# Gate and up products in float32r with second weights fetched per tile, in an attention plus mixture-of-experts kernel

## The reference

```python
x = x + layernorm(attention(layernorm(x)))      # 16 heads of 16, rope on q and k, softmax, Wo
x = x + layernorm(moe(layernorm(x)))
# moe: 8 experts, 2 per token, the two with the LARGEST distance to their centroid
d2 = |xs|^2 + |centroid|^2 - 2 xs @ centroid.T ; dist = sqrt(max(d2, 1e-12))
w, sel = top_k(dist, 2); w = softmax(w)
out += we[:, e] * ((silu(xs @ Wg[e] + bg[e]) * (xs @ W1[e] + b1[e])) @ W2[e] + b2[e])
```

## Time and profile before

| what | value |
|---|---|
| median of the three timed runs | 1595.93 us (1580.72 to 1603.84) |
| the profiled execution | 1573.55 us |
| its span, first to last instruction | 1571.8 us |
| mean granted TensorE clock | 0.96 |
| PE busy | 1435.0 us (91%) |
| DVE busy | 1110.0 us (71%) |
| ACT busy | 846.7 us (54%) |
| POOL busy | 431.5 us (27%) |
| DMA | 141.80 MB, mean 90 GB/s |
| attention groups | about 110 to 791 us of the span |
| output projection | about 794 to 876 us |
| routing | about 876 to 930 us |
| expert tiles | about 930 to 1515 us |
| end | about 1515 to 1572 us |

### The profile page before, as it was taken

The page is one execution under the profiler, slowest core; times in us unless marked ns, Lnnn a source line. Parts: engine busy times, 40 slices in busy tenths (PEclk is TensorE's granted clock), DMA queues, the critical chain, the costliest instruction groups (busy, mean ns, idle before and its releaser), DMA issues.

```text
span 1571.8 us, 29999 instructions
## 1 busy us (share of the span) xinstructions
PE 1435.0 (91%) x9435; PEld 792.5 (50%) x9436; DVE 1110.0 (71%) x1983; ACT 846.7 (54%) x1613; POOL 431.5 (27%) x417
## 2 busy tenths in 40 slices
PE   7899999999999999999999259999999999999950
PEld 5454333333333333333355136777777777777740
DVE  6989999999999999997037764555545555555425
ACT  4523888888888888887856322222222222222215
POOL 5750000000000010001024143444444444444425
PEclk9999999999999999999999659999999999999985
DMA  6986364334636454640458804222221222222236
GB/s 205 263 222 116 77 170 97 60 73 75 100 57 123 65 90 65 102 70 26 148 90 205 281 25 96 33 30 33 33 33 31 33 33 31 33 33 33 32 88 197
DMA packets 125116, 141.80 MB, mean 90 GB/s; under 512 B 55131, under 2 KB 98949, under 8 KB 125030
## 3 DMA queue, kind: packets, MB, share of 16 engines
q1 hardware_dynamic: 109126, 121.98, 33.7%
q0 software_dynamic: 15904, 18.66, 7.5%
HBM read 86.30 MB, written 54.30 MB: 89 GB/s over the span
## 4 chain that ended last, share of the span: by engine, by line
PE 79%; DVE 7%; issue 5%; ACT 4%; POOL 2%; DMA 1%; SPq 1%; DVEq 0%; POOLq 0%; ACTq 0%
PE psum L1687 21%; PE psum L1525 17%; PE psum L1551 16%; PE psum L1706 12%; PE psum L1697 3%; PE psum L1618 2%; DVE mx L955 2%; PE psum L1537 2%; ACT work L1344 1%; PE psum L1616 1%; PE psum L1499 1%; ACT weights L1354 1%; PE psum L1485 1%; PE psum L1673 1%; PE psum L1637 1%
## 5 line engine op out<-in xcount | busy, mean ns | idle before, releaser
L955 DVE TENSOR_REDUCE mx<-psum 128x1 f32<-128x1024 f32 x512 | 621.8, 1222 | 19.1 <-PE psum L1525 16.7
L1344 ACT ACTIVATE work<-psum 128x512 f32<-128x512 f32 x1024 | 556.4, 597 | 80.6 <-PE psum L1537 18.1
L1525 PE MATMUL psum<-stack 48*128 48x512 f32 x1024 | 372.9, 445 | 6.6 <-DVE mx L955 6.1
L1537 PE MATMUL psum<-stack 50*128 50x512 f32 x1024 | 375.4, 446 | 0.0
L1687 PE MATMUL psum<-weights,values 128*128 x1136 | 341.1, 453 | 0.6 <-DVE values L1174 0.6
L1551 PE MATMUL psum<-work,values 128*32 128x256 f32 x4096 | 328.6, 393 | 9.2 <-ACT weights L1354 9.2
L1687 PEld LDWEIGHTS psum<-weights,values 128*128 128x128 f32 x1136 | 211.3, 191 | 99.6 <-issue 3.1
L1525 PEld LDWEIGHTS psum<-stack 48*128 48x128 f32 x1024 | 151.3, 185 | 217.1 <-DVE mx L955 183.6
L1421 ACT ACTIVATE values<-values 128x342 f32<-128x342 f32 x142 | 69.3, 488 | 250.5 <-DVE values L1186 250.5
L1706 PE MATMUL psum<-weights,work 114*128 (+1 forms) x852 | 198.6, 383 | 1.2 <-ACT work L1432 0.8
L1551 PEld LDWEIGHTS psum<-work,values 128*32 128x32 f32 x4096 | 82.2, 108 | 197.2 <-ACT work L1344 101.2
(11 more groups left out here) (184 smaller groups left out, 1185.4 us busy)
## 6 DMA issues: line engine op xcount, KB each, us to landing
stack<-qk_scr SPq DMA_DIRECT2D x192, 128.0 KB, 6.2
qk_scr<-weights SPq DMA_DIRECT2D x16, 1024.0 KB, 4.8
weights<-in_w SPq DMA_DIRECT2D x8, 1368.0 KB, 6.6
ot_scr<-weights SPq DMA_DIRECT2D x16, 512.0 KB, 3.2
weights<-in_w SPq DMA_DIRECT2D x8, 684.0 KB
work<-in_b SPq DMA_DIRECT2D x8, 684.0 KB, 8.8
y_d<-zeros SPq DMA_DIRECT2D x1, 4224.0 KB, 14.0
v_scr<-weights SPq DMA_DIRECT2D x32, 128.0 KB, 2.4
```

What stands on the lines that cost most here:

```text
L955: dve.tensor_reduce(mx[:, r, a, t:t + 1], bank(4 + 2 * a, 2), AX, ALU.max, negate=True).then_inc(s_max, 1)
L1344: act.activation(pt[u % 4][:, j, :], bank((c + HG * u + n) % 3), ACT.Exp, scale=SC).then_inc(s_exp, 1)
L1525: ins = pe.matmul(bank(4 + 2 * a + half), qs[t3][at:at + QROWS, r, P * t:P * (t + 1)], ks[t3][at:at + QROWS, r, 512 * half:512 * (half + 1 ...
L1537: pe.matmul(bank((t3 + HG * u + n) % 3), ks[t3][at:at + MROWS, r, P * st:P * (st + 1)], qs[t3][at:at + MROWS, r, 512 * half:512 * (half + ...
```

## The change

1. **Gate and up in float32r.** x and the weights are each split into a high float32r part and a low remainder; a product is the sum of three: high x high, high x low, low x high. A tile has 3 chunks of 456 columns x 2 k blocks x 3 products: 18 float32r instructions. The bias is folded in: the last row of the weights is subtracted from all others, and since the 256 entries of x add up to zero its place is free for the bias; POOL sets the last column of `xn2` to 1 (`set_ones`). DVE's bias operations go away.
2. **Splitting the weights.** In the attention groups SP loads one expert's raw weights every second group (`load_raw`), POOL splits them (`split_weights`, after every odd group's `copy_values`), and SP stores the first six experts' parts to DRAM (`park`), from where they are loaded again during output projection, routing and the first tiles (`load_w1`, now 2.8 MB each).
3. **Second weights per tile.** They are packed into `w2_d` in DRAM and one expert's 768 KB block is fetched for each tile into one of two buffers (`stream_w2`).
4. **Transfers** of row counts that are not multiples of 16 are split into a multiple of 16 and a rest.
5. **Tile loops** of DVE, ACT and POOL are written out; the indirect DMAs read their index columns in place; there are two `x_row` and two `y_row` buffers; all of x2 comes back during the tiles.

```diff
+CG = 2 * HID // 3
+TAIL = HID - CG
+WSIZE = 2 * KC * 2 * HID
+JOBS = (3, 4, 5, 6, 7, 2, 0, 1)
+PARKED = 6
...
+        def load_raw(sp, n):
+            e = JOBS[n]
+            after(sp, s_wl, KC * n)
+            sp.dma_start(raw[:, 0, :], w1[e, 0:P, :]).then_inc(s_raw, 16)
+            for lo, hi in ((0, P - 16), (P - 16, P - 1)):
+                sp.dma_start(raw[lo:hi, 1, :], w1[e, P + lo:P + hi, :]).then_inc(s_raw, 16)
+            sp.dma_start(raw[P - 1:P, 1, :], b1[e].rearrange("(a n) -> a n", a=1)).then_inc(s_raw, 16)
+            sp.dma_start(raw[:, 2, :], w1[e, C - 1, :].partition_broadcast(P)).then_inc(s_raw, 16)
+        def park(sp, n):
+            sp.wait_ge(s_wh, KC * (n + 1))
+            sp.wait_ge(s_wl, KC * (n + 1))
+            after(sp, s_park, 16 * n)
+            sp.dma_start(w1_d[n], w1_sb[:, n % 2]...).then_inc(s_park, 16)
+        def stream_w2(sp, t, q):
+            e = sp.value_load(tile_e[0:1, bass.ds(t, 1)], min_val=0, max_val=E - 1)
+            if not isinstance(t, int) or t > 1:
+                sp.wait_ge(s_yp, t - 1)
+            sp.dma_start(w2_sb[q]..., w2_d[bass.ds(e, 1), :, :]...).then_inc(s_w2[q], 16)
...
             # SP, attention group g
                 if more:
                     load_max_rows(sp, i, c + 1, 0)
+                if g > 1 and g % 2 == 0 and g // 2 - 1 < PARKED:
+                    park(sp, g // 2 - 1)
...
                 if more:
                     load_max_rows(sp, i, c + 1, 1)
+                if g % 2 == 0:
+                    load_raw(sp, g // 2)
+                else:
+                    pack_w2(sp, g // 2)
...
             for u in range(NT // 2):
-                keep(u)
...
+                keep(u)                  # now waits for set_ones(u)
+                if u == 8:
+                    sp.wait_ge(s_vg, NG)
+                    load_w1(sp, 2)
             sp.wait_ge(s_x2, NT // 2)
-            sp.dma_start(x2_d...[:, kept:, :], x2[:, kept:, :]).then_inc(s_x2s, 16)
+            sp.dma_start(x2_d..., x2).then_inc(s_x2s, 16)
             sp.wait_ge(s_op, NT // 2)
-            for e in range(E - 3, E - 1):
-                load_w1(sp, e)
+            for n in range(2):
+                load_w1(sp, n)
             sp.wait_ge(s_x2s, 16)
-            for e in range(early):
-                load_b1(sp, e)
+            sp.wait_ge(s_dd, 1)
+            load_w1(sp, 3)
             sp.wait_ge(s_wc, 1)
             sp.dma_start(w_d[0:2 * NTOK, :]..., w_turned).then_inc(s_wd, 16)
...
+            def split_weights(n):                               # POOL
+                high, low = w1_sb[:, n % 2, 1], w1_sb[:, n % 2, 0]
+                pool.wait_ge(s_raw, 80 * (n + 1))
+                after(pool, s_park, 16 * (n - 1))
+                pool.tensor_tensor(raw[:, 0, :], raw[:, 0, :], raw[:, 2, :], ALU.subtract).then_inc(s_sub, 1)
+                pool.tensor_tensor(raw[0:P - 1, 1, :], raw[0:P - 1, 1, :], raw[0:P - 1, 2, :], ALU.subtract).then_inc(s_sub, 1)
+                for k in range(KC):
+                    pool.wait_ge(s_sub, KC * n + k + 1)
+                    pool.tensor_copy(high[:, k, :], raw[:, k, :]).then_inc(s_wh, 1)
+                for k in range(KC):
+                    pool.wait_ge(s_wh, KC * n + k + 1)
+                    pool.tensor_tensor(low[:, k, :], raw[:, k, :], high[:, k, :].bitcast(F32), ALU.subtract).then_inc(s_wl, 1)
...
                 if not (isinstance(g, int) and g + 2 >= NG):
                     copy_values(i, c + 2)
+                if g % 2 == 1:
+                    split_weights(g // 2)
                 if g in (9, 13):
                     norm_o((g - 9) // 4)
...
+            for t in range(NS):                                 # POOL, tiles
+                if t + 2 < NS:
+                    gather(t + 2)        # rows, then weights
+                if t > 0:
+                    scatter(t - 1)
...
+            def hidden(t):                                      # DVE
+                dve.wait_ge(s_si, 2 * t + 2)
+                after(dve, s_ht, t)
+                dve.tensor_tensor(hid[:, 0:TAIL], bank(1)[:, TAIL:CG], gates[:, 0:TAIL], ALU.mult).then_inc(s_hid, 1)
+                dve.wait_ge(s_gu, 3 * t + 3)
+                dve.tensor_tensor(hid[:, TAIL:HID], bank(2)[:, 0:CG], gates[:, TAIL:HID], ALU.mult).then_inc(s_hid, 1)
...
             def gate_up(t, e):                                  # PE
                 pe.wait_ge(s_mx, t + 1)
+                for c in range(3):
+                    ...
+                    dst = bank(c)[:, 0:CG]
+                    at = CG * c
                     for k in range(KC):
+                        for n, (x_part, w_part) in enumerate(((x_high, 1), (x_high, 0), (x_low, 1))):
+                            last = pe.matmul(dst, x_part[:, k, :],
+                                             w1_sb[:, bass.ds(e, 1), w_part, k, at:at + CG]...,
+                                             start=k + n == 0, stop=k + n == KC + 1)
                     last.then_inc(s_gu, 1)
```

More of the change, by code:

```diff
@@ L305, in build @@
         c = Carve(weights)
+        x2_back = c.take([NT, C])
+        c.at = 2 * WSIZE
         y_all = c.take([NT, C])
+        w1_d = nc.dram_tensor("w1_d", (PARKED, P, WSIZE), F32, kind="Internal").ap()
+        w2_d = nc.dram_tensor("w2_d", (E, P, KH * C), F32, kind="Internal").ap()
         x2_d = nc.dram_tensor("x2_d", (NTOK, C), F32, kind="Internal").ap()
@@ L864, in _ @@
             pool.wait_ge(s_wd, 32)
[L865 removed]
+            for t in range(2):
                 gather(t)
[L867 to L873 removed]
+            for t in range(NS):
[3 more added lines that the diff above has]
+                    scatter(t - 1)
+            scatter(NS - 1)
             def finish(u, p):
                 pool.wait_ge(s_fn, 2 * u + 2)
[L877 removed]
+                both = [v[:, bass.ds(2 * u, 2), :] for v in (y_all, x2_back)]
                 pool.tensor_tensor(both[0], both[0], both[1], ALU.add).then_inc(s_fo, 1)
@@ L1431, in save_ht @@
                 after(act, s_yp, t)
-                act.activation(h_t.rearrange("p k t -> p (k t)")[0:KP, 0:4 * P], bank(4)[0:KP, :], ACT.Copy).then_inc(s_hta, 1)
-            gate(0)
-            save_ht(0)
-            gate(1)
-            save_y(0)
-            save_ht(1)
-            with act.Fori(2, NS) as t:
+                act.activation(h_t.rearrange("p k t -> p (k t)")[0:KP, 0:4 * P], bank(4)[0:KP, :], ACT.Copy).then_inc(s_hts, 1)
+            for t in range(NS):
                 gate(t)
-                save_y(t - 1)
+                if t > 0:
+                    save_y(t - 1)
                 save_ht(t)
@@ L1698, in turn_hidden, with down @@
                 last.then_inc(s_ht, 1)
-            def down(t, e):
-                pe.wait_ge(s_hta, t + 1)
-                pe.wait_ge(s_htd, t + 1)
+            def down(t, q, loads):
+                pe.wait_ge(s_hts, 2 * (t + 1))
+                pe.wait_ge(s_w2[q], 16 * loads)
                 after(pe, s_yr, t)
@@ L1705, in down @@
                     rows = KP + 1 if k == 0 else KP
-                    last = pe.matmul(bank(7)[:, 0:C], h_t[0:rows, k, :],
-                                     w2_sb[0:rows, bass.ds(e, 1), k, :].rearrange("p a n -> p (a n)"),
+                    last = pe.matmul(bank(7)[:, 0:C], h_t[0:rows, k, :], w2_sb[q][0:rows, k, :],
                                      start=k == 0, stop=k == KH - 1)
```

343 lines of the change are left out of this document (153 added, 190 removed).

## The result

The changed kernel takes 1654.36 us (median of four runs, 1647.78 to 1662.78) against 1588.33 for the kernel before (four runs, 1577.26 to 1603.84): a ratio of 1.044, 95% interval 1.034 to 1.054, so **slower by 4.4%**. The profiled execution took 1647.78 us, its span is 1646.0 against 1571.8, and the mean granted clock 0.91 against 0.96.

A forecast was written before the change was run, and what follows sets the result against it. DVE was taken to bound attention, PE's instruction stream the expert tiles. 109 (attention) - 65 + 4 + 1.5 - 6 = +43.5 us, put on the mean of four executions (1588.5), gave 1632 us; range 1592 to 1685, at 60%.

The forecast's parts named there:

- The stall: Attention: POOL's 15.1 us split job, less 2.83 us slack in five groups, holds DVE seven times; +91.6 us.
- The clock: Attention: each of six new stalls loses 2.94 us to a lower granted clock; +17.6 us.
- Gate and up: Expert tiles: 18 float32r products at 0.205 us replace 4.60 us of float32 passes, 0.91 us less a tile; -65 us.
- The projection: Output projection: keep waits for set_ones, ACT's layernorm for keep, a 2.8 MB load ahead of one store; +4 us.
- Routing: Routing to first gather: extra loads just hidden; small conversion, weight gather and second DVE operation before the first tile; +1.5 us.
- the end: End of kernel: SP issues 8 loads instead of 12 before telling DVE; -6 us.
- the job was not cheap: Rival, attention: POOL's job is cheaper than its rows say, attention pays little; 1522 to 1583 us, 20%.
- the loads don't show: Rival, gate and up: float32r weight loads show, costing 76 us more instead of 65 less; 1773 us, 4%.
- the tiles aren't held: Rival, expert tiles: row gathers beside the weight fetch keep the tile at 8.07 us; 1697 us, 7%.
- The one of late maxima: Rival, attention: park's 2.8 MB store ahead of load_max_rows(.., 1) delays maxima 8 us in six groups, +48; 1680 us, 9%.

The follow-up runs named there:

- e2: Changed kernel with the weight split moved from behind copy_values to behind split_max(g + 1, 0) in odd groups; 1565.54 us, ratio 0.979 to the kernel before.
- e3: Changed kernel with only the two row subtractions (6.2 us) left behind copy_values, the rest of the split moved to the next even group; 1590.32 us, ratio 0.999.
- e7: e2's kernel with gate and up as one float32 product of the high parts, low parts left out; 1611.78 us (two runs), tile 8.06 us.
- e8: e2's kernel without the third product (low x high), 12 float32r matmuls a tile instead of 18; 1487.95 us (two runs), tile 5.96 us.
- e12: e6's kernel with keep not waiting for set_ones (255 columns stored and gathered) and placed ahead of its step's loads; 1504.87 us, ratio 0.949.
- e5: e2's kernel with norm_o also moved, behind the first half of the maxima in groups 10 and 14; 1551.73 us, ratio 0.977.
- e6: e5's kernel with park moved into the odd group, behind all rows of maxima; 1525.85 us, ratio 0.964, attention 654.2 us.
- e11: e6's kernel with the split back behind copy_values in group 7 alone; 1552.66 us in a single run, attention 688.8 us.
- e4: Changed kernel with the last batch's loads of o at u = 1 and its inverses at u = 2, instead of both at 4; 1653.87 us, ratio 1.041.

## Why the prediction was right

The kernel became slower, and the time lies in the range, 22 us above the forecast. The stages of the two profiles add up to +74.9 us where the sum had 43.5, so the steps together were 31 us short, nearly all of it at half clock and in the wait of the projection. By its steps:

- **The stall** (+91.6): right. 92.6 us in seven waits, of which 3.8 were there before, so 88.8 new; the job was 14.7 us instead of 15.1. It rested on one pattern that was in the trace already, `norm_o` at the same place, with its slack of 2.83 us. e2 and e3 show the same rule with no job and with one of 6.2 us.
- **The clock** (+17.6): too small. The seven stalled groups lost 30.7 us, 4.4 each, where I took the 2.94 of one short stall. On top, the first group lost 9.7 us in a stretch at half clock that stands in the profiles of all variants of the change (13.7 to 37.5 us long where it can be told apart, 3.4 before), with no wait that explains it. With the 2.9 us that the kernel before lost at the earlier trace rows taken off, the term measures 37.5. The two terms make 88.8 + 37.5 = 126.3 of the 129.1 us.
- **Gate and up** (-65): right. 0.211 us for 456 columns instead of the 0.205 read off, 0.91 predicted and 0.88 us found in a tile. e7 and e8 show that it is the product's format, and that PE alone holds the tile down to 5.96 us. With 0.19 us of weight load at each of 18 products that start every 0.211 us, the loads don't show. By a rule of the Trainium skill ("TensorE: Matmul & The Clock Gate", Part 3, The mechanism: a load overlaps a running matmul only where the row groups differ) each would have been exposed; the trace of the changed kernel contradicts it, as that of before did.
- **The projection** (+4): too small. I had it within 0 to 8 us and it is 16.2. The path through `keep` was named, but as a wait only, and with the wrong thing ahead of the store: `set_ones` and the 2.8 MB load. What held it in the trace were the 16 loads that the change put ahead of it, with the ones set 3.4 us earlier. It is 5.8 us of wait and then 20.5 us at half clock, which at 0.42 lost per microsecond is 8.6, 14.4 together. e12 took the wait away; the part at half clock differs from profile to profile with this code (in e2 it was 3.4 us, and the stage 89.6).
- **Routing** (+1.5) and **the end** (-6): 0.2 and -7.2.
- **The rivals.** Three fell: the job was not cheap, the loads don't show, the tiles aren't held. The one of late maxima didn't show in the changed kernel, where PE never waited a microsecond for `stack<-m_scr`. It appeared once the long stalls of the odd groups were gone: `park` there cost e5 31.8 us of attention against e6, of which 6.4 are waits and the rest is clock. The mechanism was priced at 48, and by the length of the transfers alone.

What stays open: why the first group's stretch at half clock is longer in every variant of the change, why a stall of about 12 us goes with 17 us at half clock in one place and with 34 in another (from 247.6 in the profile after), why some waits of 1.4 to 1.5 us bring no stretch at all, and the slow stages ahead of attention in e8.

## What to carry to other kernels

Before a job goes on an engine that is "27% busy", look at who stands behind the place where it is queued, and take the slack from a job that already stands there. Seven jobs of 14.7 us came with 92.6 us of waits ahead of `split_max(.., 0)`, and behind it with only the 3.8 us that `norm_o` had cost before. When a bound engine is made to wait, price the clock with it, for short waits too, and look which small wait comes forward when the large one is gone: here POOL's job hid the transfer ahead of the maxima. And when a change moves a store in a queue, count the loads that now stand ahead of it.

## What the runs showed of the hardware

- The granted clock fell to half at waits of only 1.4 to 2.1 us of an otherwise full PE (e2, e5, e11), as well as at those of 12 us. But one wait of 1.4 us in e2, one of 1.5 in e5 and one of 1.5 in the kernel before went without a fall. In attention it stayed there for 10.2 us (e3) to 44.4 us (e4), while PE worked on, where the kernel before shows 3.4 and 6.8.
- POOL converts 1368 columns of float32 to float32r in 1.34 us (mean of 16 in the changed kernel), or 0.98 ns a column, and subtracts as many in 3.10 us: 2.27 ns.
- A float32r product of 456 columns takes 0.211 us, or 0.463 ns a column (the changed kernel); a float32 product of as many (two passes) 0.765 us, or 0.84 ns a column and pass (e7). Three of the one cost 0.633, so they are cheaper than one of the other.
